# Second cross attention: projections and output tiles placed inside the attention waves

## The reference, cut to what matters

```python
x = x + _L1_attn_ref(_layernorm(x, axis=-1), ...)
x = x + _L1_xattn_ref(_layernorm(x, axis=-1), ctx_512, L1_xattn_Wq, L1_xattn_Wkv_expand, L1_xattn_Wout)
x = x + _L1_ffn_ref(_layernorm(x, axis=-1), ...)

def _L1_xattn_ref(q, latent_kv, Wq, Wkv_expand, Wout):     # 16 heads of 32
    qp = q @ Wq.T
    kv = latent_kv @ Wkv_expand.T                          # 128 features -> K and V of 512
    k, v = jnp.split(kv, 2, axis=-1)
    scores = jnp.einsum('bhqd,bhkd->bhqk', qh, kh) * inv_sqrt_d
    scores = jnp.where(causal, scores, jnp.finfo(scores.dtype).min)
    attn = jax.nn.softmax(scores, axis=-1)
    out = jnp.einsum('bhqk,bhkd->bhqd', attn, vh)
    return out.transpose(0, 2, 1, 3).reshape(b, sq, H) @ Wout.T
```

## Time and profile before

| | before |
|---|---|
| median of 3 runs | 1651.32 us (1651.06 to 1651.63) |
| span of the profiled execution | 1651.2 us |
| PE busy | 1590.1 us, 96% |
| PEld busy | 1353.0 us, 82% |
| DVE busy | 942.8 us, 57% |
| ACT busy | 731.2 us, 44% |
| POOL busy | 665.9 us, 40% |

### The profile page before, as it was taken

One profiled execution on the slowest core, in us unless ns is written; L12 is line 12 of the kernel. 1 busy time (PEld: TensorE's weight loads), 2 busy tenths in 40 slices (PEclk: granted clock), 3 DMA queues, 4 the chain that ended last, 5 costly groups with the idle time before them and its releaser, 6 DMA issues.

```text
span 1651.2 us, 24551 instructions
## 1 busy us (share of the span) xinstructions
PE 1590.1 (96%) x9832; PEld 1353.0 (82%) x9832; DVE 942.8 (57%) x1535; ACT 731.2 (44%) x1227; POOL 665.9 (40%) x483
## 2 busy tenths in 40 slices
PE   7999999989999999989999989998989999999998
PEld 7898666878899998768889976887668888888887
DVE  6555664366545455677768566354766455554554
ACT  3113655322587765666511156332635334353342
POOL 3875542441498873421137633212512422222321
PEclk9999999999999999999999999999999999999999
DMA  4110003123222007200001100110001111111111
GB/s 166 52 65 28 2 2 116 56 84 127 95 89 65 14 1 267 93 1 1 1 13 65 51 27 1 50 39 32 21 23 43 45 64 46 51 46 51 51 58 45
DMA packets 28580, 88.52 MB, mean 54 GB/s; under 512 B 4154, under 2 KB 4282, under 8 KB 28215
## 3 DMA queue, kind: packets, MB, share of 16 engines
q1 hardware_dynamic: 28468, 86.96, 15.4%
HBM read 85.11 MB, written 1.84 MB: 53 GB/s over the span
## 4 chain that ended last, share of the span: by engine, by line
PE 83%; DVE 8%; ACT 5%; issue 3%; POOL 1%; ACTq 0%; DVEq 0%; POOLq 0%
PE PS L261 19%; PE PS L263 18%; PE PS L262 18%; PE PS L266 7%; PE PS L1125 4%; PE PS L1462 3%; PE PS L1477 2%; PE PS L561 2%; PE PS L952 1%; PE PS L585 1%; PE PS L1709 1%; PE PS L1697 1%; PE PS L551 1%; DVE sm L1731 1%; PE PS L569 1%
## 5 line engine op out<-in xcount | busy, mean ns | idle before, releaser
L307 POOL TENSOR_TENSOR HL<-stg,HL 128x1024 fp32r<-128x1024 f32 (+2 forms) x111 | 243.8, 2199 | 543.5 <-ACT HL L302 525.5
L261 PE MATMUL PS<-XT,HL 128*128 128x448 f32 x608 | 225.0, 370 | 4.3 <-DVE XT L342 3.7
L263 PE MATMUL PS<-XT,HL 128*128 128x448 f32 x608 | 223.1, 367 | 0.0
L262 PE MATMUL PS<-XT,HL 128*128 128x448 f32 x608 | 223.1, 367 | 0.0
L302 ACT ACTIVATE HL<-stg 128x1024 fp32r<-128x1024 f32 (+2 forms) x111 | 104.5, 944 | 216.6 <-PE PS L263 200.9
L261 PE MATMUL PS<-HL,XT 128*128 128x512 f32 (+1 forms) x380 | 137.8, 363 | 2.2 <-DVE XT L1981 1.4
L263 PE MATMUL PS<-HL,XT 128*128 128x512 f32 (+1 forms) x380 | 134.8, 355 | 0.0
L262 PE MATMUL PS<-HL,XT 128*128 128x512 f32 (+1 forms) x380 | 134.8, 355 | 0.0
L261 PEld LDWEIGHTS PS<-XT,HL 128*128 128x128 f32 x608 | 115.0, 189 | 16.6 <-DVE XT L342 4.9
L262 PEld LDWEIGHTS PS<-XT,HL 128*128 128x128 f32 x608 | 115.1, 189 | 9.2
L263 PEld LDWEIGHTS PS<-XT,HL 128*128 128x128 f32 x608 | 114.9, 189 | 9.2
(11 more groups left out here) (299 smaller groups left out, 3813.7 us busy)
## 6 DMA issues: line engine op xcount, KB each, us to landing
stg<-in_wst SPq DMA_DIRECT2D x87, 512.0 KB, 3.2
stg<-in_wst SPq DMA_DIRECT2D x16, 352.0 KB, 3.0
stg<-in_wst SPq DMA_DIRECT2D x16, 320.0 KB, 3.2
wsum<-in_wfc SPq DMA_DIRECT2D x8, 512.0 KB, 3.7
wsum<-in_wpj SPq DMA_DIRECT2D x8, 512.0 KB, 3.5
raw<-in_wfc SPq DMA_DIRECT2D x8, 512.0 KB, 7.5
stg<-in_wst SPq DMA_DIRECT2D x16, 256.0 KB, 2.6
raw<-in_wpj SPq DMA_DIRECT2D x7, 512.0 KB, 7.0
```

Source lines behind the costliest of these rows:

```text
L261: e.matmul(out, lh, rh, start=start, stop=False)
L262: e.matmul(out, lh, rl, start=False, stop=False)
L263: return e.matmul(out, ll, rh, start=False, stop=stop)
L307: e.tensor_tensor(slot(k)[:, 1, 0:n], stg[k % NSTG][:, 0:n], slot(k)[:, 0, 0:n].bitcast(F), A.subtract).then_inc(*done("pool_w", k))
```

## The change

Half of the projections (the queries and keys of the second half of the tokens, and the values of sequences 2 to 7) and the output tiles 0 to 3 are issued inside the waves. They all go through one bank, 7 (`FILL`), and `values` keeps bank 6 alone. `pe_q2` now begins with the keys of the first half. The residual and statistics of tiles 0 to 3 are taken on DVE inside the waves, the rest of their norm in `dve_o2`. `KC`, the split context, lies in another part of SBUF, since it is now read while the waves use its old place. The rounds of o2 0, o2 1 and of the MoE's first piece move from behind `act_q2` and waves 1 and 2 to waves 2, 4 and 8.

```diff
+        def query2(e, u, bank):
+            half, i, e_ = u // 4, u // 2 % 2, u % 2
+            k = piece["q2", i][0]
+            if half == 0 and e_ == 0:
+                has_w(e, k)
+            project(e, slot(k), 128 * e_, half, bank).then_inc(*done("pe_q2", "q", u))
+            if half and e_:
+                freed[k] = "pe_q2", "q", u
+
+        def query2_out(e, u, bank):
+            half, i, e_ = u // 4, u // 2 % 2, u % 2
+            e.wait_ge(*upon("pe_q2", "q", u))
+            e.activation(q_at(half, 0, 2 * i + e_), psv(bank), ACT.Copy).then_inc(*done("act_q2", u))
+
+        def key2(e, c, half, bank):
+            w = slot(piece["kv2", 0][0])
+            mm3(e, PS[:, bank, 0:HT], w[:, 0, c * 128:(c + 1) * 128], w[:, 1, c * 128:(c + 1) * 128],
+                KC[:, 0, 4 * half:4 * half + 4, :], KC[:, 1, 4 * half:4 * half + 4, :], True, True).then_inc(*done("pe_q2", "k", c, half))
+
+        def value2(e, b, bank):
+            k = piece["kv2", 0][0]
+            w = slot(k)
+            mm3(e, PS[0:S, bank, :], KC[:, 0, b, :], KC[:, 1, b, :], w[:, 0, 512:1024], w[:, 1, 512:1024], True,
+                True).then_inc(*done("pe_q2", "v", b))
+            if b == NB - 1:
+                freed[k] = "pe_q2", "v", b
+
+        def value2_out(e, b, bank):
+            e.wait_ge(*upon("pe_q2", "v", b))
+            e.tensor_copy(V2[:, b, :], PS[0:S, bank, :]).then_inc(*done("dve_q2", "v", b))
...
+        K_BANK, Q_BANK = (7, 0, 1, 2), (3, 7, 0, 1)
         def pe_q2(e):
...
+            has_w(e, piece["kv2", 0][0])
+            e.wait_ge(*upon("dve_o1", "kc"))
+            for c in range(4):
+                if c:
+                    e.wait_ge(*upon("dve_ln", "ln2", K_BANK[c], "lo"))
+                key2(e, c, 0, K_BANK[c])
+            e.wait_ge(*upon("dve_ln", "ln2", 3, "lo"))
+            for u in range(4):
+                if u:
+                    e.wait_ge(*upon("act_q2", "k", u - 1))
+                query2(e, u, Q_BANK[u])
+                if u == 1:
                     ln_turn(e, "ln2", NT - 1, xn[0], NT - 1)
...
+            value2(e, 0, 2)
+            e.wait_ge(*upon("dve_ln", "ln2", 4, "lo"))
+            value2(e, 1, 4)
...
         def pe_att2(e):
...
+            def ahead(w):
+                if w < 4:
...
+                    query2(e, 4 + w, FILL)
+                elif 4 < w < 9:
+                    e.wait_ge(*upon("dve_q2", "v", w - 1))
+                    output2(e, w - 5, FILL)
+
+            def between(w):
+                if w < 4:
+                    e.wait_ge(*upon("act_q2", 4 + w))
+                    key2(e, w, 1, FILL)
+                elif w == 4:
+                    e.wait_ge(*upon("dve_q2", "v", 3))
+                    value2(e, 4, FILL)
+                elif w < 8:
+                    e.wait_ge(*upon("dve_o2", "x", w - 5))
+                    value2(e, w, FILL)
+
+            def behind(w):
+                if w in (2, 3):
+                    e.wait_ge(*upon("dve_q2", "k", w, 1))
+                    value2(e, w, FILL)
+
+            e.wait_ge(*upon("dve_q2", "v", 1))
...
                 if w > 1:
                     turn8(e, "a2", 2 * w - 3)
+                ahead(w)
                 if w < NB:
                     less(2 * w)
                 if w > 1:
+                    e.wait_ge(*upon("dve_q2", "v", w - 2))
                     values(w - 2)
+                between(w)
                 if w < NB:
                     less(2 * w + 1)
                 if 0 < w <= NB:
                     turn8(e, "a2", 2 * w - 2)
+                behind(w)
...
         def dve_att2(e):
...
                 if w < NB:
                     largest(2 * w)
+                if 4 < w < 9:
+                    residual(e, "o2", w - 5, FILL)
+                if w < NB:
                     largest(2 * w + 1)
+                if w < 4:
+                    e.wait_ge(*upon("pe_q2", "k", w, 1))
+                    e.tensor_copy(K2[:, w, HT:2 * HT], PS[:, FILL, 0:HT]).then_inc(*done("dve_q2", "k", w, 1))
+                elif w < 8:
+                    value2_out(e, w, FILL)
...
+                if 4 < w < 9:
+                    stats2(e, w - 5)
                 if w < NB:
                     sum8(e, "a2", 2 * w)
+                if w in (2, 3):
+                    value2_out(e, w, FILL)
...
+        def output2(e, t, bank):
+            for c in range(4):
+                k = piece["o2", c // 2][0]
+                if t == 0 and c % 2 == 0:
+                    has_w(e, k)
+                s, o = slice(t * P, (t + 1) * P), c % 2 * 512
+                last = mm3(e, PS[:, bank, :], XT[:, 0, c, s], XT[:, 1, c, s], slot(k)[:, 0, o:o + 512], slot(k)[:, 1, o:o + 512],
+                           c == 0, c == 3)
+            last.then_inc(*done("pe_o2", "t", t))
+            if t == NT - 1:
+                for i in range(2):
+                    freed[piece["o2", i][0]] = "pe_o2", "t", t
+        def stat(t):
+            return ((q6[:, t, :], qmv[:, t, :], qrs[:, t, :]) if t < 4 else
+                    (st6[:, t % 2, 0, :], mv[:, t % 2, :], rs[:, t % 2, :]) if t < 6 else (st6[:, 0, 1, :], mvl[:, 0, :], rsl[:, 0, :]))
+        def stats2(e, t):
+            s6, m, r = stat(t)
+            e.bn_stats(s6, x[:, t, :]).then_inc(*done("dve_ln", "lne", t, "st"))
+            e.wait_ge(*upon("dve_ln", "lne", t, "st"))
+            e.bn_aggr(m, s6).then_inc(*done("dve_ln", "lne", t, "mv"))
+        def norm2(e, t):
+            s6, m, r = stat(t)
+            e.wait_ge(*upon("act_ln", "lne", t, "root"))
+            e.reciprocal(r[:, 2:3], r[:, 1:2]).then_inc(*done("dve_ln", "lne", t, "rstd"))
+            e.wait_ge(*upon("dve_ln", "lne", t, "rstd"))
+            e.tensor_scalar(RES[:, t, :], x[:, t, :], m[:, 0:1], r[:, 2:3], A.subtract, A.mult).then_inc(*done("dve_ln", "lne", t, "xn"))
+        def root2(e, t):
+            s6, m, r = stat(t)
+            e.wait_ge(*upon("dve_ln", "lne", t, "mv"))
+            e.activation(r[:, 1:2], m[:, 1:2], ACT.Sqrt, bias=eps[:, 0:1], scale=1.0).then_inc(*done("act_ln", "lne", t, "root"))
...
         def pe_o2(e):
-            pe_out(e, "o2", "o2", 4, "lne", lambda t: RES[:, t, :], None, skip_last=True, lows=lambda c: upon("dve_a2", "lo", NB - 1))
+            for t in range(4, NT):
+                e.wait_ge(*upon("dve_a2", "lo", NB - 1 if t == NT - 1 else t + 1))
...
+                output2(e, t, t)
+                if t > 4:
+                    ln_turn(e, "lne", t - 5, RES[:, t - 5, :], t - 5)
+            for t in range(2, NT - 1):
+                ln_turn(e, "lne", t, RES[:, t, :], t)
+            e.wait_ge(*upon("dve_ln", "lne", 3, "lo"))
 
         def act_o2(e):
...
+            for t in range(4):
+                root2(e, t)
+            root2(e, 4)
+            ln_hi(e, "lne", 0, 0)
+            root2(e, 5)
+            ln_hi(e, "lne", 1, 1)
+            root2(e, 6)
+            for t in range(2, NT - 1):
+                ln_hi(e, "lne", t, t)
+                if t == 3:
                     for k in (1, 2):
                         round_w(e, first_up + k)
...
         def dve_o2(e):
...
+            e.wait_ge(*upon("pe_a2", "sc", NB - 1, 3))
+            norm2(e, 0)
+            residual(e, "o2", 4)
+            stats2(e, 4)
+            norm2(e, 1)
+            residual(e, "o2", 5)
+            stats2(e, 5)
+            ln_lo(e, "lne", 0, 0)
+            norm2(e, 2)
+            residual(e, "o2", 6)
+            stats2(e, 6)
+            ln_lo(e, "lne", 1, 1)
+            for t in range(3, NT):
+                norm2(e, t)
+                ln_lo(e, "lne", t - 1, t - 1)
```

More of the change, by code:

```diff
@@ L1818, in pool_o1 @@
                 rest_w(e, k)
-        def pe_q2(e):
[L1823 to L1830, removed]
-                    ln_turn(e, "ln2", NT - 1, xn[0], NT - 1)
[L1832 to L1849, removed]
@@ L1851, in act_q2 @@
-        def act_q2(e):
-            for u in range(8):
-                half, i, e_ = u // 4, u // 2 % 2, u % 2
-                if u == 4:
-                    ln_hi(e, "ln2", NT - 1, NT - 1)
-                e.wait_ge(*upon("pe_q2", "q", u))
-                e.activation(q_at(half, 0, 2 * i + e_), psv(u), ACT.Copy).then_inc(*done("act_q2", u))
-            round_w(e, piece["o2", 0][0])
+        def query2(e, u, bank):
[6 more added lines that the diff above has]
+                freed[k] = "pe_q2", "q", u
@@ L1860, in dve_q2 @@
+        def act_q2(e):
+            for c in range(4):
+                e.wait_ge(*upon("pe_q2", "k", c, 0))
+                e.activation(K2[:, c, 0:HT], PS[:, K_BANK[c], 0:HT], ACT.Copy).then_inc(*done("act_q2", "k", c))
+            query2_out(e, 0, Q_BANK[0])
+            query2_out(e, 1, Q_BANK[1])
+            ln_hi(e, "ln2", NT - 1, NT - 1)
+            query2_out(e, 2, Q_BANK[2])
+            query2_out(e, 3, Q_BANK[3])
         def dve_q2(e):
             ln_lo(e, "ln2", NT - 1, NT - 1)
-            for u in range(8):
-                c, half = u // 2, u % 2
```

(23 more changed lines are left out.)

42 lines of the change are left out of this document (25 added, 17 removed).

## The result

| | before | changed |
|---|---|---|
| first comparison, median | 1651.32 us (1650.76 to 1652.89, 9 runs) | 1655.24 us (1653.23 to 1660.99, 9 runs) |
| ratio to before, 95% interval | | 1.0025 [1.0015, 1.0035] |
| repeated with the last experiments | 1651.77 us (21 runs) | 1657.95 us (1655.41 to 1660.71, 5 runs) |
| ratio, 95% interval | | 1.0033 [1.0021, 1.0046] |

The change makes the kernel slower by 0.25% and, repeated on another chip, by 0.33%: 3.9 and 6.2 us between the medians. I had forecast 1650.8, no change.

The account below looks back on a forecast made before the run. PE, busy 96% of the span, was taken as the bound. About 21 us of present losses to win stood against new holes and low clocks: the path gave 1651.3, the count 1649.4, the forecast 1650.8 us, range 1646 to 1655.5.

Parts of the forecast that it names:

- two new holes: PE waits 5.9 us for kv2 at the start of `pe_q2`, and for DVE's norms between tile 6 and the MoE.
- hole for kv2, keys start: Start of `pe_q2`: PE free at 1111.68 waits for POOL's rest of kv2 until 1117.6, 5.9 us.
- clock behind it: Half speed after each hole: 2.5 us lost behind kv2's, 2.2 on the MoE's first matmuls; 0 to 3.4 each.
- waves 0, 1: Each gets a query and a key unit; with waits for ACT's copy and the second exponential, 6.4 and 7.9 us.
- waves 2 to 7: Fills added to a steady wave's 5.72 us, PE setting the pace: 9.7, 9.7, 6.9, then 9.4 each.
- waves 8 and 9: Transposes, output tile 3, `values` and waits of 1.15 and 1.05: 9.7 us, ending at 1213.5, at full clock.
- tile 6's end to MoE: DVE's remaining statistics, norms and rests hold PE 6.3 us, plus 1.0 for a norm delayed by POOL's rest: 7.3.
- My path of 1651.3: Sum following each wait: MoE 2.2 us earlier, 2.2 lost to the clock behind it, so 1651.3 unchanged.
- the count of losses: Cross-check over the stages touched: work 96.5 plus new losses 21.8 makes 118.3 against 120.2, 1.9 gained, 1649.4.
- a sign of being wrong: Waves 5 to 7 taking over 10 us would show the forecast wrong, with the bank or DVE the bound.
- A third fall of the clock: Rival: waves 8 and 9 lower the clock, the work behind loses 1.7 to 3.4 us, 1652.5 to 1654.2; chance 0.12.
- the single bank: Rival: fills queue for bank 7 in waves 0 to 7, half a microsecond each, 4 us, 1654.8; chance 0.14.

Follow-up runs that it names:

- the last experiments: Later runs; beside them the changed kernel was run again unaltered: 1657.95 us, ratio 1.0033 to the kernel before.
- the last kernel: Changed kernel with two query units in the first hole, both waits removed, wave 9 filled and the tail reordered: 1634.02 us, ratio 0.989 to the kernel before.

## Why the prediction was wrong

The mechanism was right: waves filled, two new holes, a low clock behind each. Its marks against the first trace:

| step | predicted | measured |
|---|---|---|
| hole for kv2, keys start | 5.9, 1117.6 | 5.55, 1117.51 |
| clock behind it | 2.5 | 2.6 |
| first scores | 1135.0 | 1135.31 |
| waves 0, 1 | 6.4, 7.9 | 7.6, 7.5 |
| waves 2 to 7 | 9.7, 9.7, 6.9, 9.4 each | 9.3, 9.1, 6.9, 10.45, 8.95, 8.95 |
| waves 0 to 7 | 68.8 | 68.65 |
| waves 8 and 9 | 9.7, to 1213.5 | 11.1, to 1215.06 |
| tile 6's end to MoE | 7.3 | 7.4 |
| MoE's first matmul | 1229.6 | 1231.22 |
| clock behind it | 2.2 | 2.35 |

Added up as in the prediction, the losses before are 21.1 us (2.2, 11.9 and 0.1 without a matmul, 6.9 for the clock). In the changed kernel they are 6.3, 3.5 and 7.7 without a matmul by the windows above, and 2.6 and 2.35 (half of 4.70, an estimate) for the clock: 22.5. The difference of 1.4 is near that of the stage lengths, 127.68 - 126.05 = 1.63. So the trade of my forecast took place, and ended 1.6 us on the wrong side in the first profile. Three steps failed.

1. **"a time worked out from the trace is compared with 1651.3 directly."** The span leaves out 1.75 us of the device time, and the execution traced was some 1.6 above its kernel's median, since its clock was low up to 47.6, which it was not in the next (that one has a fall from 739.2 to 742.6 instead, which gives back a part). The two cancelled in the number that I looked at. My path of 1651.3 was a span: it stands for a device time of 1653.05. The changed kernel's first trace (1654.79) is 1.8 above the estimated 1652.95 of the trace before, and the other 2 of the 3.9 us between the medians are the 1.6 by which the trace before lay above its median, and 0.45 from 1654.79 to 1655.24. Another 0.5 is what I took off the path for the count of losses, which was the worse of the two.

2. **The sum of waves 5 and 8.** Two waits on the path were missing. Wave 5 has one of 1.24 us for the rest of o2 1. The diff shows its round moved behind wave 4, and its first reader in wave 5; I looked at what the fills need of banks, and not at what they need of weights, as I had done for kv2. In the sum it was covered, with 0.8 too little for waves 0 and 1, by waves 2, 3, 6 and 7, each 0.4 to 0.6 shorter than predicted: that the sum of waves 0 to 7 was right is luck. Wave 5 at 10.45 also met a sign of being wrong that I had given (over 10), and the cause was neither the bank nor DVE, as I had written there, but POOL's rest. Wave 8 has one of 1.20 ahead of its transposes, of the kind that the earlier trace rows show; my sum counts wave 9's waits only. By these rows the two are 2.4 us, more than the 1.6 by which the MoE came late, and the steps of the sum behind them fit (tail 7.4 for 7.3, clock 2.35 for 2.2). With both removed the kernel takes the time of before, at 1.0001.

3. **"A third fall of the clock", as something that a kernel has or hasn't.** I gave it 0.12. Wave 9 had it in four profiles, one of them of the unaltered changed kernel, which in its other profile was without it; wave 1 had one in four, and there again the unaltered kernel shows both. A median holds a share of each. The two falls of the kernel before in this stage came in both of its traces.

What stays open is how much of the median the falls hold. In the second profile of the changed kernel those of waves 1 and 9 make 3.1 us, and the medians agree with a part of it: five kernels, in which the first hole is kept at a full clock, or the tail is reordered, or one or both waits are gone, stand at 1.0001 to 1.0006, 3 us and more under the changed kernel, for edits that save 1.2 to 3.8 by their rows. Falls ahead of the stage count as well: the kernel before begins it at 1111.3 and 1109.5, the changed one at 1111.3 and 1111.6. Whether the changed kernel begins it later on average, or by chance in these traces, is not shown; two profiles of each kernel don't give the share.

Of the rivals, the single bank was not the cause: between query, key and value the waits are 0.25 and less. Normalizations on DVE took longer beside POOL's rests, as forecast: by 0.8 and 1.25 us beside the two, of which the first is ahead of the MoE; I had taken 1.0.

## What to carry to other kernels

Work moved into waves leaves holes where it stood. Ask of each end what is queued there now, and which slower engine's work (here a split of weights, a chain of norms) it had been hiding; and move the next pieces, or that engine's order, in the same change: the same idea lost 0.25% alone and won 1.1% with both ends and the last waves filled. List for each moved operation every operand, weights included, and not the bank alone. Before setting a sum against a median, set the traced execution's device time against that median, and look where its clock fell, ahead of the stage too.

## What the runs showed of the hardware

- 26 matmuls whose result nobody reads made the stage 2.6 us shorter: the granted clock was 0.50 behind the hole of 5.5 us in each of the eight profiles that have the hole, and 1.00 behind it once it was filled.
- A fall behind a short wait is no constant of the program: wave 1 at 1.00 in one execution and 0.61 in another, 1.4 us; wave 9 the same, 1.6 us.
- A fall costs less where it lies under waits: from the MoE's first matmul to the router's it was 7.9 us with the fall from 1232.9 on, and 6.6 with one from 1226.2 on, of which PE waited a part.
- In the last kernel, with 103.95 of 107.84 us busy, there is no fall in the stage.
